# Two layers of the experts: 128-row blocks against 256-row items whose products run in float32r parts

## The chip, the cores and the metric

The kernel runs on one core of a Trainium2 chip, as one launch. The metric is the device time of that launch in microseconds, lower is better. Five engines work beside one another, each on its own list of instructions and joined by semaphores: TensorE (PE in the profile, with its weight loads as PEld), VectorE (DVE), ScalarE (ACT), GpSimd (POOL) and SyncE (SP), which here issues most DMAs.

## The reference, cut to what matters

A decoder layer on 4 batches of 1024 rows with 256 columns, all in float32: self-attention with 16 heads, cross-attention on 77 rows of context, and a mixture of 8 experts of which each row takes its best two. The change is in the experts:

```python
x = x + _L0_attn_ref(_layernorm(x), ...)
x = x + _L0_xattn_ref(_layernorm(x), ctx_1024, ...)
flat_x = _layernorm(x).reshape(-1, 256)          # 4096 rows
logits = flat_x @ W_router + b_router            # 8 experts
top_vals, top_idx = jax.lax.top_k(logits, 2)
for e in range(8):
    h = jax.nn.relu(flat_x @ W1[e] + b1[e])      # W1[e]: 256 x 1024
    y = h @ W2[e] + b2[e]                        # W2[e]: 1024 x 256
    final_output = final_output + y * w[:, None] # w: 0 where the row did not choose e
```

## The kernel before, in words

Attention comes first, batch by batch, and fills TensorE to about 1080 us. Its rows are routed as they are done: the normalised rows are scattered to a table in device memory (`expert_rows`), one region for each expert. 4096 rows with two experts each are 64 blocks of 128 rows when they divide evenly; since each expert rounds up, the kernel has 71 blocks (`NBLK`). The first 40 (`EARLY`) are taken from batches 0 to 2, so that they can run while the second half of batch 3 is still in its cross-attention and routing; a table computed on DVE says for each block which expert and which rows it has.

A block n is these steps, each on one engine:

- `load` (SP): the block's rows into `xi`, and its expert's first weights, 1 MB, into one of three buffers `w1_now`. All eight second weights were brought into `w2` (8 MB) during attention (`prefetch`).
- `xi_turn` (PE), `xi_turned` (ACT): the rows turned, so that columns lie on partitions.
- `up` in two halves (PE): the first layer in plain float32, 32 matmul instructions of 128 columns (one float32 product is two instructions). `hid_fore` (ACT) and `hid_aft` (DVE) add the bias and cut at zero, one half each.
- `down` (PE): the second layer. Blocks 0 to 21 have it in plain float32, 16 instructions of 256 columns. From block 22 (`FINE`) it is a sum of float32r products: a number is split in a high part (rounded to float32r) and the low rest, and high*high + high*low + low*high are summed, 24 instructions of 256 columns. For that `hid_high` (ACT) and `hid_low` (DVE) split the rows, and `w2_high` (ACT) and `w2_low` (DVE) split the weights of each block.
- `yo` (DVE): the product times the row's routing weight, with the bias; `added` (POOL): an indirect DMA that adds 128 rows to the output in device memory. From block 22 POOL computes the routing weight too (`yo_weight`).

The order on each engine is fixed when the kernel is built: the generator `plan()` adds steps to one list, and each engine takes its kinds of steps from it in that order. `TAKES` (line 78) holds the planner's costs of the steps. `blocks()` (line 530) interleaves the steps of blocks n, n+1 and n+2; while batch 3 is being completed, its steps stand between those of `blocks()`. An engine that waits for a semaphore holds everything that stands behind it in its list.

Two kinds of subtraction carry the low parts, both from tensors in SBUF: on DVE (line 1921)

```python
e.tensor_tensor(w2_low[n % NPARTS][:, chunks, :], second_layer(expert, chunks), w2_high[n % NPARTS][:, chunks, :].bitcast(F32), ALU.subtract)
```

and, once at the start of the kernel for 512 columns of the attention weights, on POOL (line 1980, `w_low_late`).

## Time and profile before

| | us |
|---|---|
| median of 3 runs | 1608.52 (1606.69 to 1613.93) |
| profiled execution, first to last instruction | 1607.6 |
| first `xi_turn` (line 1383) | 1081.9 |
| last plain second layer (line 1421) ends | 1274.9 |
| last `yo` (line 1935) starts | 1596.2 |
| `added`, from issue to landing (median, 1300 to 1600 us) | 5.4 |
| PE busy | 1552.3 (97%) |
| DVE busy | 1189.6 (74%) |
| ACT busy | 934.6 (58%) |
| POOL busy | 387.4 (24%) |

The profile page has no time for the profiled execution beside its span; what lies around a span is the difference between the runs' median and it, 0.9 us. The page lists each engine's busy time, and the chain of work that ended last, followed back from the end: 90% of that chain is PE. Stretches of the span can be asked for by window, and each group of instructions by line and shape.

### The profile page before, as it was taken

How to read it: one execution, taken by the hardware profiler on the slowest of the kernel's cores; microseconds unless marked ns; L12 is line 12 of the kernel's file. 1: busy time of each engine (PE TensorE's matmuls, PEld its weight loads, DVE VectorE, ACT ScalarE, POOL GpSimd, SP SyncE). 2: the span in 40 equal slices, each digit the busy share in tenths (PEclk: the TensorE clock that was granted, in tenths of full speed). 3: DMA queues.
4: the chain of work that ended last, by engine and by line, in shares of the span. 5: the costliest groups of instructions: out<-in, count | busy, mean ns of one | idle time of the engine just before them, and what ended most of it. 6: DMA issues, size and time to landing. Idle time of an engine off the chain costs nothing.

```text
span 1607.6 us, 31234 instructions
## 1 busy us (share of the span) xinstructions
PE 1552.3 (97%) x10542; PEld 963.5 (60%) x10542; DVE 1189.6 (74%) x2409; ACT 934.6 (58%) x1786; POOL 387.4 (24%) x462
## 2 busy tenths in 40 slices
PE   5899999999999999999999999999999999999997
PEld 3433443344554444445434443439999999999997
DVE  5888878888877788787877777713354788888885
ACT  3156656677556767664765756772222466666663
POOL 6201120002110041210013100142134334344443
PEclk9799999999999999999999999999999999999998
DMA  6561351232151450314414333234556666766763
GB/s 181 110 126 24 74 122 23 23 43 34 38 99 52 70 86 13 44 41 83 70 51 73 44 106 132 68 130 128 158 179 204 190 199 198 208 191 199 210 192 102
DMA packets 92672, 173.41 MB, mean 108 GB/s; under 512 B 13236, under 2 KB 51124, under 8 KB 92385
## 3 DMA queue, kind: packets, MB, share of 16 engines
q1 hardware_dynamic: 75376, 143.69, 35.2%
q0 software_dynamic: 15744, 26.54, 7.6%
q8 instruction: 85, 1.39, 0.4%
q10 hardware_dynamic: 1392, 1.18, 0.4%
...
## 4 chain that ended last, share of the span: by engine, by line
PE 90%; DVE 4%; ACT 2%; issue 2%; DMA 1%; POOL 0%; SPq 0%; ACTq 0%; DVEq 0%; POOLq 0%
PE ps L1395 16%; PE ps L1183 15%; PE ps L1209 14%; PE ps L1169 13%; PE ps L1138 8%; PE ps L1421 5%; PE ps L1281 2%; PE ps L1315 2%; PE ps L1212 2%; DVE rmax L1632 2%; PE ps L1172 2%; ACT prob L1439 1%; PE ps L1228 1%; PE ps L1383 1%; PE ps L1296 1%
## 5 line engine op out<-in xcount | busy, mean ns | idle before, releaser
L1632 DVE TENSOR_REDUCE rmax<-ps 128x1 f32<-128x512 f32 x960 | 621.2, 685 | 175.4 <-PE ps L1212 86.4
L1439 ACT ACTIVATE prob<-ps 128x512 f32<-128x512 f32 x1024 | 560.8, 601 | 308.2 <-PE ps L1169 157.7
L1209 PE MATMUL ps<-stacked_k,stacked_q 112*128 112x512 bf16 x1024 | 392.1, 390 | 11.4 <-DVE rmax L1629 3.8
L1169 PE MATMUL ps<-stacked_q,stacked_k 115*128 115x512 bf16 x1024 | 358.7, 381 | 3.0 <-ACT prob L1439 1.6
L1183 PE MATMUL ps<-prob,values 128*32 128x512 f32 x2048 | 273.6, 606 | 6.8 <-ACT prob L1439 6.8
L1395 PE MATMUL ps<-xiT,w_now 128*128 128x128 f32 x2272 | 267.5, 275 | 0.0
L1209 PEld LDWEIGHTS ps<-stacked_k,stacked_q 112*128 112x128 bf16 x1024 | 99.5, 99 | 279.2 <-DVE rmax L1632 184.2
L1395 PEld LDWEIGHTS ps<-xiT,w_now 128*128 128x128 f32 x2272 | 262.7, 192 | 1.3
L1169 PEld LDWEIGHTS ps<-stacked_q,stacked_k 115*128 115x128 bf16 x1024 | 97.7, 98 | 152.1 <-ACT prob L1439 67.9
L2060 POOL DMA_INDIRECT out<-yo,xi x71 | 114.9, 1618 | 244.6 <-DVE yo L1935 219.8
L1559 ACT ACTIVATE hidT<-ps,b 128x128 f32<-128x128 f32 x284 | 80.1, 364 | 97.0 <-PE ps L1395 97.0
L1904 DVE TENSOR_SCALAR hidT<-ps,b 128x128 f32<-128x128 f32 x284 | 80.2, 345 | 53.4 <-PE ps L1395 43.8
L1921 DVE TENSOR_TENSOR w_low<-w,w_high 128x2048 fp32r<-128x2048 f32 x49 | 112.3, 2293 | 5.9 <-issue 4.3
L1138 PE MATMUL ps<-w_high,hid_high 128*128 128x256 f32 x392 | 114.1, 291 | 0.0
L1569 ACT ACTIVATE hid_high<-hidT 128x512 fp32r<-128x512 f32 x98 | 62.1, 634 | 89.4 <-DVE hidT L1904 87.7
L1212 PE MATMUL ps<-ramps,slopes 128*128 128x128 f16 x512 | 113.3, 221 | 0.0
L1172 PE MATMUL ps<-ramps,slopes 128*128 128x128 f16 x512 | 112.4, 219 | 0.0
L1138 PE MATMUL ps<-w_high,hid_low 128*128 128x256 f32 x392 | 110.1, 281 | 0.0
L1138 PE MATMUL ps<-w_low,hid_high 128*128 128x256 f32 x392 | 110.1, 281 | 0.0
L1581 ACT ACTIVATE w_high<-w 128x2048 fp32r x49 | 93.7, 1913 | 16.8 <-issue 15.8
L1961 POOL TENSOR_TENSOR rstd_of<-varp,minus_half 128x8 f32<-128x8 f32 (+1 forms) x14 | 21.3, 1520 | 333.4 <-DVE varp L1680 333.4
L2020 POOL DMA_INDIRECT expert_rows<-xn,slot x64 | 62.1, 971 | 160.9 <-ACT prob L1439 128.6
...
## 6 DMA issues: line engine op xcount, KB each, us to landing
w_now<-in_w SPq DMA_DIRECT2D x71, 1024.0 KB, 5.3
...
w<-in_w SPq DMA_DIRECT2D x8, 1024.0 KB, 9.2
...
xr<-in_x POOLq DMA_DIRECT2D x4, 1024.0 KB, 9.8
```

The source lines that it names most:

```text
L1138: last = e.matmul(ps[:, bank, 0:D], rows[n % 2][:, c, :], weights[n % NPARTS][:, c, :], start=(c == 0 and i == 0), stop=(c == FC - 1 and i ...
L1169: m = e.matmul(ps[:, bank, :], ka[i][0:ROWS, hh, kt * P:(kt + 1) * P], qa[i][0:ROWS, hh, ch * BANK:(ch + 1) * BANK], start=True, stop=True)
L1172: m = e.matmul(ps[:, bank, (kt % 4) * P:(kt % 4 + 1) * P], slopes[:, g * HG + hh, :], ramps[:, kt % 2, :], start=False, stop=True, skip_gr ...
L1183: m = e.matmul(ps[CT * hh:CT * (hh + 1), AV_BANK, :], vt[b % 2][:, kt, c0:c0 + CT], prob[:, unit_of(G, ch, kt, hh) % NPROB, :], start=(kt ...
L1209: m = e.matmul(ps[:, bank, :], qa[i][0:MAX_ROW, hh, qt * P:(qt + 1) * P], ka[i][0:MAX_ROW, hh, kc * BANK:(kc + 1) * BANK], start=True, sto ...
L1212: m = e.matmul(ps[:, bank, (qt % 4) * P:(qt % 4 + 1) * P], slopes[:, g * HG + hh, :], ramps[:, 1 - qt % 2, :], start=False, stop=True, ski ...
L1395: m = e.matmul(ps[:, 1 + 2 * (n % 2) + half, q * P:(q + 1) * P], w1_now[n % NW][:, c, f * P:(f + 1) * P], xiT[n % 2][:, c, :], start=(c == ...
L1439: e.activation(prob[:, u % NPROB, :], ps[:, score_bank(u), :], ACT.Exp).then_inc(sem["exp"], 1)
L1581: e.activation(w2_high[n % NPARTS][:, :, :], second_layer(expert, slice(0, FC)), ACT.Copy).then_inc(sem["w2_high"], 1)
L1632: e.tensor_reduce(rmax[:, G % 2, hh * NT + qt, kc:kc + 1], ps[:, p.bank("max", *k), :], AX.X, ALU.max).then_inc(sem["maxed"], 1)
L1921: e.tensor_tensor(w2_low[n % NPARTS][:, chunks, :], second_layer(expert, chunks), w2_high[n % NPARTS][:, chunks, :].bitcast(F32), ALU.subt ...
L2060: e.indirect_dma_start(t["out"], bass.IndirectOffsetOnAxis(ap=xi[n % NX][:, TOKEN:TOKEN + 1].bitcast(I32), axis=0), yo[n % NY][:, :], None ...
```

## The change

The 71 blocks become 39 items: 32 of 256 rows (pairs) and 7 of 128 rows (singles). Items 0 to 16 are pairs and are taken from batches 0 to 2; of the other 22, items 20, 23, 26, 29, 32, 35 and 38 are singles. In a pair both layers are sums of three float32r products: `up` is four quarters of 12 instructions with 256 columns, `down` is 24 instructions of 256 columns for each of its two tiles. The split of the rows before the first layer is new (`xi_high` on ACT, `xi_low` on DVE, 128x512 each), and so is the split of the first weights (`w1_high` on ACT, `w1_low` on POOL, 128x2048 each, for every pair). `hid_high` and `hid_low` cover 128x1024 in one instruction, `hid_fore` and `hid_aft` 128x256. A single has both layers in plain float32 and splits nothing. The second weights are no longer prefetched; each item loads its 1 MB of first and 1 MB of second weights (3 and 2 buffers). The weights lie in device memory so that a partition reads 8 KB in one piece. `yo` computes the routing weight itself on DVE for every tile, and POOL's `yo_weight` is gone. The table step on DVE is rewritten for pairs and singles.

```diff
+NX, NY, N1, N2, NH2 = 4, 2, 3, 2, 2
...
+EARLY = -(-((NB - 1) * S * TOPK - NE * (PAIR - 1)) // PAIR)
+LATE = NBLK - 2 * EARLY
+SINGLES = NE - 1
+PAIRS_LATE = (LATE - SINGLES) // 2
+assert 2 * PAIRS_LATE + SINGLES == LATE
...
+    tiles, unit = [2] * EARLY, [2 * n for n in range(EARLY)]
+    pairs, singles = iter(range(PAIRS_LATE)), iter(range(SINGLES))
+    for n in range(PAIRS_LATE + SINGLES):
+        alone = n % 3 == 0 and n > 0
+        tiles.append(1 if alone else 2)
+        unit.append(2 * EARLY + (2 * PAIRS_LATE + next(singles) if alone else 2 * next(pairs)))
+    return tiles, unit
...
+    def split_first(n):
+        if TILES[n] == 2:
+            add("w1_high", n)
+            add("w1_low", n)
...
+    def split_second(n):
+        if TILES[n] == 2:
+            add("w2_high", n)
+            add("w2_low", n)
...
+    def up_quarter(n, q):
+        add("up", n, q)
+        add(("hid_fore", "hid_aft")[q % 2], n, q)
...
     def blocks():
-        turn_block(0)
-        turn_block(1)
+        split_first(0)
+        turn_item(0)
         yield
-        for half in range(2):
-            up_half(0, half)
+        split_first(1)
+        turn_item(1)
+        yield
+        for q in range(4):
+            up_quarter(0, q)
+            if q % 2:
+                split_rows(0, q // 2)
             yield
-        for n in range(NBLK):
-            if n + NW < NBLK:
-                add("load", n + NW)
-            if n + 1 < NBLK:
-                for half in range(2):
-                    up_half(n + 1, half)
-                    if n + 1 >= FINE and half == 0:
+        add("load_1", N1)
+        split_second(0)
+        split_first(2)
+        for n in range(NITEM):
+            for q in range(4):
+                if n + 1 < NITEM:
+                    up_quarter(n + 1, q)
+                    if q == 1:
                         split_rows(n + 1, 0)
                     yield
-            if n + 2 < NBLK:
-                turn_block(n + 2)
-            if FINE <= n + NPARTS - 1 < NBLK and n + 1 > FINE:
-                add("w2_low", n + NPARTS - 1)
-            if FINE <= n + 1 < NBLK:
+            if n + 4 < NITEM:
+                assert n + 4 != EARLY or ("table", 1, TABLE_PARTS - 1) in p.number
+                add("load_1", n + 4)
+            if n + 2 < NITEM:
+                turn_item(n + 2)
+            if n + 1 < NITEM:
                 split_rows(n + 1, 1)
-            add("down", n)
-            add("yo", n)
-            if FINE <= n + 1 < NBLK:
-                assert n == FINE - 1 or ("table", 1, TABLE_PARTS - 1) in p.number
-                add("yo_weight", n + 1)
-            if n == NBLK - 1:
-                add("last_front")
-            add("added", n)
-            if FINE <= n + NPARTS < NBLK:
-                assert ("scatter", NB - 1, NT - 1, TOPK - 1) in p.number
-                add("w2_high", n + NPARTS)
-                if n + NPARTS < FINE + 2:
-                    add("w2_low", n + NPARTS)
-            yield
+            if n + 3 < NITEM:
+                split_first(n + 3)
+            for tt in range(TILES[n]):
+                add("down", n, tt)
+                if tt == 0 and n + 1 < NITEM:
+                    split_second(n + 1)
+                yield
+            for tt in range(TILES[n]):
+                add("yo", n, tt)
+                add("added", n, tt)
+            if n + 2 < NITEM:
+                add("load_2", n + 2)
+            if n + NX < NITEM:
+                assert n + NX != EARLY or ("zeros", NE - 1) in p.number
+                add("load_x", n + NX)
...
+                elif kind == "load_1":
+                    n, = k
...
+                    if n == 2:
+                        e.wait_ge(sem["attend"], attend_of(LAST, NCH - 1, NT - 1))
+                    elif n >= N1:
+                        e.wait_ge(sem["up"], p.upto("up", n - N1, 3))
+                    of = e.value_load(expert_of[0:1, UNIT[n]:UNIT[n] + 1], min_val=0, max_val=NE - 1)
+                    e.dma_start(w1_now[n % N1][:, :, :], t["w1"][bass.ds(of, 1)].rearrange("a p c f -> p (a c) f")).then_inc(sem[f"w1_in{n % N1}"], 16)
+                elif kind == "load_2":
+                    n, = k
+                    if n >= N2:
+                        e.wait_ge(sem["down"], p.upto("down", n - N2, last_tile(n - N2)))
+                    of = e.value_load(expert_of[0:1, UNIT[n]:UNIT[n] + 1], min_val=0, max_val=NE - 1)
+                    e.dma_start(w2_now[n % N2][:, :, :], t["w2"][bass.ds(of, 1)].rearrange("a p c f -> p (a c) f")).then_inc(sem[f"w2_in{n % N2}"], 16)
+                elif kind == "load_x":
...
                         landed(e, n - NX)
-                    at = e.value_load(row_of[0:1, n:n + 1], min_val=0, max_val=NROW - P)
-                    e.dma_start(xi[n % NX][:, :], rows_in[bass.ds(at, P), :]).then_inc(sem[f"slots_in{n % NX}"], 16)
-                    if n >= NW:
-                        e.wait_ge(sem["up"], p.upto("up", n - NW, 1))
-                    if n >= 2:
-                        first_layer(n)
+                    for tt in range(TILES[n]):
+                        at = e.value_load(row_of[0:1, UNIT[n] + tt:UNIT[n] + tt + 1], min_val=0, max_val=IDLE)
+                        e.dma_start(xi[n % NX][tt][:, :], rows_in[bass.ds(at, P), :]).then_inc(sem[f"slots_in{n % NX}"], 16)
 
         @block.tensor
         def _(e):
-            def down_in_parts(n, bank):
...
+                    if q == 0 and TILES[n] == 2:
+                        e.wait_ge(sem["xi_low"], p.upto("xi_low", n))
+                        e.wait_ge(sem["w1_low"], p.upto("w1_low", n))
+                    elif q == 0:
+                        e.wait_ge(sem["xi_high"], p.upto("xi_high", n))
+                        e.wait_ge(sem[f"w1_in{n % N1}"], 16 * (n // N1 + 1))
+                    for f in (2 * q, 2 * q + 1):
+                        cols = slice(f * P, (f + 1) * P)
+                        into = ps[:, 1 + q, f % 2 * PAIR:f % 2 * PAIR + TILES[n] * P]
                         for c in range(DC):
-                            m = e.matmul(ps[:, 1 + 2 * (n % 2) + half, q * P:(q + 1) * P], w1_now[n % NW][:, c, f * P:(f + 1) * P],
-                                         xiT[n % 2][:, c, :], start=(c == 0), stop=(c == DC - 1))
+                            if TILES[n] == 2:
+                                high, low = xT_high[n % 2][:, c, :], xT_low[n % 2][:, c, :]
+                                e.matmul(into, w1_high[n % NH2][:, c, cols], high, start=(c == 0), stop=False)
+                                e.matmul(into, w1_high[n % NH2][:, c, cols], low, start=False, stop=False)
+                                m = e.matmul(into, w1_low[n % N1][:, c, cols], high, start=False, stop=(c == DC - 1))
+                            else:
+                                m = e.matmul(into, w1_now[n % N1][:, c, cols], xT_one[n % 2][:, c, :], start=(c == 0), stop=(c == DC - 1))
                     m.then_inc(sem["up"], 1)
...
+                    if TILES[n] == 2:
+                        if tt == 0:
+                            e.wait_ge(sem["w2_low"], p.upto("w2_low", n))
+                        for c in range(FC):
+                            if tt == 0 and c % (FC // 2) == 0:
+                                e.wait_ge(sem["hid_low"], p.upto("hid_low", n, c // (FC // 2)))
+                            high, low = hid_high[n % 2][:, c, tile_of(tt)], hid_low[n % 2][:, c, tile_of(tt)]
+                            e.matmul(into, high, w2_high[n % NH2][:, c, :], start=(c == 0), stop=False)
+                            e.matmul(into, high, w2_low[n % N2][:, c, :], start=False, stop=False)
+                            m = e.matmul(into, low, w2_high[n % NH2][:, c, :], start=False, stop=(c == FC - 1))
                     else:
...
+                elif kind == "w1_high":
+                    n, = k
...
+                    e.wait_ge(sem[f"w1_in{n % N1}"], 16 * (n // N1 + 1))
+                    if n >= NH2:
+                        e.wait_ge(sem["up"], p.upto("up", n - NH2, 3))
+                    e.activation(w1_high[n % NH2][:, :, :], w1_now[n % N1][:, :, :], ACT.Copy).then_inc(sem["w1_high"], 1)
...
+                elif kind == "xi_low":
+                    n, = k
+                    e.wait_ge(sem["xi_high"], p.upto("xi_high", n))
+                    rows = ps[:, 0, 0:DC * PAIR].rearrange("p (c r) -> p c r", c=DC)
+                    e.tensor_tensor(xT_low[n % 2][:, :, :], rows, xT_high[n % 2][:, :, :].bitcast(F32), ALU.subtract).then_inc(sem["xi_low"], 1)
...
+                    e.tensor_tensor(w2_low[n % N2][:, :, :], w2_now[n % N2][:, :, :], w2_high[n % NH2][:, :, :].bitcast(F32),
                                     ALU.subtract).then_inc(sem["w2_low"], 1)
...
-                elif kind == "yo_weight":
+                elif kind == "w1_low":
...
+                    e.wait_ge(sem["w1_high"], p.upto("w1_high", n))
+                    e.tensor_tensor(w1_low[n % N1][:, :, :], w1_now[n % N1][:, :, :], w1_high[n % NH2][:, :, :].bitcast(F32),
+                                    ALU.subtract).then_inc(sem["w1_low"], 1)
...
+                    e.wait_ge(sem["yo"], p.upto("yo", n, tt))
+                    if tt == 0 and n:
                         landed(e, n - 1)
-                    e.indirect_dma_start(t["out"], bass.IndirectOffsetOnAxis(ap=xi[n % NX][:, TOKEN:TOKEN + 1].bitcast(I32), axis=0),
-                                         yo[n % NY][:, :], None, compute_op=ALU.add).then_inc(sem[f"added{n % 2}"], 16)
-            landed(e, NBLK - 2)
-            landed(e, NBLK - 1)
+                    e.indirect_dma_start(t["out"], bass.IndirectOffsetOnAxis(ap=xi[n % NX][tt][:, TOKEN:TOKEN + 1].bitcast(I32), axis=0),
+                                         yo[n % NY][tt][:, :], None, compute_op=ALU.add).then_inc(sem["landed"], 16)
+            landed(e, NITEM - 1)
 
```

The lists of three engines show the change in the steady part. First DVE, between one split of second weights and the next; before, `w2_low` is line 1921, `hid_low` 1913, `yo` 1935 and the 128x128 rows of 1904 are `hid_aft`:

```order
L1921 TENSOR_TENSOR w2_low2<-w2,w2_high2 128x2048
L1913 TENSOR_TENSOR hid_low1<-hidT1,hid_high1 128x512
...
L1933 TENSOR_SCALAR bias0<-b2_all,weight0 128x256
L1935 SCALAR_TENSOR_TENSOR yo0<-ps,weight0,bias0 128x256
L1913 TENSOR_TENSOR hid_low0<-hidT0,hid_high0 128x512
...
L1904 TENSOR_SCALAR hidT0<-ps,b1 128x128
...
L1904 TENSOR_SCALAR hidT0<-ps,b1 128x128
...
L1904 TENSOR_SCALAR hidT0<-ps,b1 128x128
...
L1904 TENSOR_SCALAR hidT0<-ps,b1 128x128
...
L1921 TENSOR_TENSOR w2_low0<-w2,w2_high0 128x2048
```

Now, over one pair (`hid_aft` is line 1981, `hid_low` 1988, `xi_low` 1969, `w2_low` 1993, `yo` with its bias 2005 and 2007):

```order
L1981 TENSOR_SCALAR hid0<-ps,b1 128x256
...
L1981 TENSOR_SCALAR hid0<-ps,b1 128x256
L1988 TENSOR_TENSOR hid_low0<-hid0,hid_high0 128x1024
...
L1981 TENSOR_SCALAR hid0<-ps,b1 128x256
...
L1981 TENSOR_SCALAR hid0<-ps,b1 128x256
L1969 TENSOR_TENSOR xT_low1<-ps,xT_high1 128x512
L1988 TENSOR_TENSOR hid_low0<-hid0,hid_high0 128x1024
L1993 TENSOR_TENSOR w2_low0<-w2_now0,w2_high0 128x2048
...
L2005 TENSOR_SCALAR bias0<-b2_all,weight0 128x256
L2007 SCALAR_TENSOR_TENSOR yo10<-ps,weight0,bias0 128x256
...
L2005 TENSOR_SCALAR bias1<-b2_all,weight1 128x256
L2007 SCALAR_TENSOR_TENSOR yo11<-ps,weight1,bias1 128x256
```

The split of the second weights stood ahead of the last split of the rows; now it is behind both, directly ahead of the two `yo` of the item before. Then ACT, before (`hid_fore` 1559, `hid_high` 1569, `xi_turned` 1545, `w2_high` 1581):

```order
L1569 ACTIVATE hid_high1<-hidT1 128x512
L1545 ACTIVATE xiT0<-ps 128x256
L1569 ACTIVATE hid_high1<-hidT1 128x512
...
L1581 ACTIVATE w2_high0<-w2 128x2048
...
L1559 ACTIVATE hidT0<-ps,b1 128x128
...
L1559 ACTIVATE hidT0<-ps,b1 128x128
...
L1559 ACTIVATE hidT0<-ps,b1 128x128
...
L1559 ACTIVATE hidT0<-ps,b1 128x128
L1569 ACTIVATE hid_high0<-hidT0 128x512
L1545 ACTIVATE xiT1<-ps 128x256
L1569 ACTIVATE hid_high0<-hidT0 128x512
```

and now, from one `w2_high` (line 1627) to the next, with `w1_high` 1621, `hid_fore` 1640, `hid_high` 1648 and `xi_high` 1612:

```order
L1627 ACTIVATE w2_high0<-w2_now0 128x2048
...
L1640 ACTIVATE hid1<-ps,b1 128x256
...
L1640 ACTIVATE hid1<-ps,b1 128x256
L1648 ACTIVATE hid_high1<-hid1 128x1024
...
L1640 ACTIVATE hid1<-ps,b1 128x256
...
L1640 ACTIVATE hid1<-ps,b1 128x256
L1612 ACTIVATE xT_high0<-ps 128x512
L1648 ACTIVATE hid_high1<-hid1 128x1024
L1621 ACTIVATE w1_high1<-w1_now0 128x2048
L1627 ACTIVATE w2_high1<-w2_now1 128x2048
```

Two conversions of 128x2048 stand behind one another, first the first weights of the item two further on, then the second weights of this one. Last POOL, the end of its list before (`added` is line 2060, the routing weight 1591 to 1595):

```order
L2060 DMA out<-yo1,xi0 4224x256
...
L1591 TENSOR_SCALAR weight1<-xi2,code_of 128x1
L1592 TENSOR_TENSOR weight1<-weight1,xi2 128x1
L1595 TENSOR_TENSOR weight1<-weight1,xi2 128x1
L2060 DMA out<-yo0,xi1 4224x256
```

and now the first pairs (`w1_low` is line 2098, `added` 2112, 2033 and 2083 belong to batch 3):

```order
L2098 TENSOR_TENSOR w1_low0<-w1_now0,w1_high0 128x2048
L2098 TENSOR_TENSOR w1_low1<-w1_now1,w1_high1 128x2048
L2083 TENSOR_TENSOR xr<-xr,xbo_all 128x256 x4
L2098 TENSOR_TENSOR w1_low2<-w1_now2,w1_high0 128x2048
L2033 TENSOR_TENSOR rstd_of0<-varp0,minus_half 128x4
L2098 TENSOR_TENSOR w1_low0<-w1_now0,w1_high1 128x2048
L2112 DMA out<-yo00,xi00 4224x256
L2112 DMA out<-yo01,xi01 4224x256
L2083 TENSOR_TENSOR xr<-xr,xbo_all 128x256 x4
L2098 TENSOR_TENSOR w1_low1<-w1_now1,w1_high0 128x2048
L2112 DMA out<-yo10,xi10 4224x256
L2112 DMA out<-yo11,xi11 4224x256
```

A 128x2048 subtraction per pair has come into POOL's list, ahead of the two `added` of an item.

## Rows read from the trace of the kernel before

**Rows 1.** Page, part 1: busy us (share of the span) and instructions.

```profile
PE 1552.3 (97%) x10542; PEld 963.5 (60%) x10542; DVE 1189.6 (74%) x2409; ACT 934.6 (58%) x1786; POOL 387.4 (24%) x462
```

**Rows 2.** Chain that ended last, in order of time: start us, us, what.

```profile
1216.89 3.57 PE ps L1395 x32
1220.68 3.46 PE ps L1421 x16
1224.14 3.57 PE ps L1395 x32
...
1298.54 2.84 PE ps L1138 x24
1301.38 3.57 PE ps L1395 x32
1305.17 2.84 PE ps L1138 x24
```

**Rows 3.** Windows: length, then busy us (instructions) by engine, clock, DMA share, GB/s.

```profile
1110.00:1270.00 160.00, 160.00 (x1102) 150.00 (x1102) 75.58 (x291) 43.69 (x122) 51.57 (x41) 1.00 0.60 179
1300.00:1400.00 100.00, 100.00 (x877) 100.00 (x876) 82.57 (x138) 67.15 (x120) 42.34 (x63) 1.00 0.67 199
```

**Rows 4.** Groups by line and shape, ACT: xcount, busy us, mean ns, idle before.

```profile
L1581 ACT ACTIVATE w_high<-w 128x2048 fp32r x49 | 93.7, 1913 | 16.8 <-issue 15.8 <-PE ps L1138 0.9
...
L1569 ACT ACTIVATE hid_high<-hidT 128x512 fp32r<-128x512 f32 x98 | 62.1, 634 | 89.4 <-DVE hidT L1904 87.7
```

**Rows 5.** The same for DVE.

```profile
L1921 DVE TENSOR_TENSOR w_low<-w,w_high 128x2048 fp32r<-128x2048 f32 x49 | 112.3, 2293 | 5.9 <-issue 4.3
L1904 DVE TENSOR_SCALAR hidT<-ps,b 128x128 f32<-128x128 f32 x284 | 80.2, 345 | 53.4 <-PE ps L1395 43.8 <-issue 5.2 <-DVE landed_of L1890 0.9
L1913 DVE TENSOR_TENSOR hid_low<-hidT,hid_high 128x512 fp32r<-128x512 f32 x98 | 67.7, 691 | 44.2 <-ACT hid_high L1569 44.2
```

**Rows 6.** Timeline of DVE around one `yo`: start us, us, instruction.

```profile
1105.49 1.13 DVE L1904 TENSOR_SCALAR hidT<-ps,b 128x128 f32<-128x128 f32 x4 [1.08 <-PE ps L1395]
...
1106.55 0.22 DVE L1588 SCALAR_TENSOR_TENSOR weight<-xi,code_of 128x1 f32<-128x1 f32 x1
...
1107.12 0.35 DVE L1933 TENSOR_SCALAR bias<-b_all,weight 128x256 f32 x1 [0.15 <-DVE weight L1595]
...
1109.09 0.48 DVE L1935 SCALAR_TENSOR_TENSOR yo<-ps,weight,bias 128x256 f32<-128x256 f32 x1 [1.62 <-PE ps L1421]
```

**Rows 7.** Line 1607 on POOL: duration ns min/median/max, first and last start.

```profile
L1607 POOL TENSOR_TENSOR q_part<-rest_of,q_part x14: 1152/1157/1167, 34.3 to 717.8; 128x512 bf16<-128x512 f32 x14
```

**Rows 8.** Line 2006 on POOL, 256 columns, same columns.

```profile
L2006 POOL TENSOR_TENSOR xr<-xr,bo_all x32: 711/728/739, 226.7 to 1076.4; 128x256 f32<-128x256 f32 x32
```

**Rows 9.** Line 1607 on DVE, same columns.

```profile
L1607 DVE TENSOR_TENSOR q_part<-rest_of,q_part x2: 693/694/694, 21.4 to 27.0; 128x512 bf16<-128x512 f32 x2
```

**Rows 10.** Line 1592 on POOL, one column wide, same columns.

```profile
L1592 POOL TENSOR_TENSOR weight<-weight,xi x49: 189/190/2290, 1276.8 to 1593.0; 128x1 f32<-128x1 f32 x49
```

**Rows 11.** Timeline at 27 us, POOL and DVE at once.

```profile
27.11 3.17 POOL L1980 TENSOR_TENSOR wqkv_low<-xn,wqkv_high 128x512 fp32r<-128x512 f32 x2
...
29.16 1.67 DVE L1607 TENSOR_TENSOR k_part<-rest_of,k_part 128x512 bf16<-128x512 f32 x1
```

**Rows 12.** Timeline at 1340 us, DVE and POOL at once.

```profile
1340.86 2.29 DVE L1921 TENSOR_TENSOR w_low<-w,w_high 128x2048 fp32r<-128x2048 f32 x1
...
1340.92 2.28 POOL L1592 TENSOR_TENSOR weight<-weight,xi 128x1 f32<-128x1 f32 x1
```

**Rows 13.** Windows where attention ends and the blocks begin, columns as in rows 3.

```profile
1076.00:1082.00 6.00, 3.19 (x22) 2.23 (x18) 0.75 (x3) 3.14 (x6) 1.08 (x2) 1.00 0.39 79
1082.00:1090.00 8.00, 7.53 (x46) 6.81 (x44) 0.69 (x1) 2.88 (x8) 2.78 (x4) 0.79 0.38 140
```

**Rows 14.** DMA from 1300 to 1600 us: queue and loads to landing.

```profile
q1 hardware_dynamic: 17874, 50.80, 49.3%
...
w_now<-in_w SPq DMA_DIRECT2D x43, 1024.0 KB, 5.4
```

506 lines of the change are left out of this document (242 added, 264 removed).

## The prediction

> **What bounds the kernel now.** I read the busy times first: PE works 97% of the span, DVE 74%, ACT less [rows 1]. That is a mean over two parts, so I asked for windows in the part that changes. From 1300 to 1400 us PE is busy without a gap and at full clock, DVE 83 of 100 us, ACT 67 [rows 3]. The chain of waits there is PE alone, and its starts repeat: 7.25 us for a block with a plain float32 second layer (1216.89 to 1224.14), 6.63 us for one with float32r parts (1298.54 to 1305.17) [rows 2]. So 22 blocks of 7.25 and 49 of 6.63 make 484 us, and every us that PE is spared is gained as long as PE stays the engine waited for. DVE has only 17 us in 100 to spare.
>
> **PE: what is removed.** A float32r product with 256 columns takes 2.84 / 24 = 0.118 us [rows 2]. A pair has 48 of them for each layer and four turning products of about 0.11 (what lies between a first layer's end and the second's start: 1305.17 - 1301.38 - 3.57 = 0.22 for two): 96 x 0.118 + 0.44 = 11.8 us, against 14.5 for two early blocks and 13.3 for two late ones. A single is the old plain block, 7.25. Sum 32 x 11.8 + 7 x 7.25 = 428 us, **56 us less** than 484. That holds only if the others deliver a pair in 11.8 us.
>
> **Do they? The loop through DVE, ACT and POOL.** The lists are in order, so I follow them from the end of one item's last `yo` to the end of the next item's, and price each step.
>
> - `hid_aft` quarter 1 of the next item but one, two instructions of 256 columns. One of 128 takes 0.345, four 1.13 [rows 5, 6], so the spacing is 0.26; DVE needs (2293 - 691) / 1536 = 1.04 ns for a column [rows 5], so 128 more columns cost 0.13: 0.39 + 0.48 = 0.9 us.
> - `hid_high` of half 0 waits for it: 128x1024 on ACT, 0.634 + 512 x 0.833 ns (from 634 and 1913 ns) [rows 4] = 1.06.
> - `hid_low` of half 0 waits for that: 0.69 + 0.53 = 1.22 [rows 5].
> - `hid_aft` quarter 3, behind it on DVE: 0.9.
> - `hid_high` of half 1: 1.06. On DVE `xi_low` runs beside it.
> - `w1_high`, 128x2048 behind it on ACT: 1.91 [rows 4].
> - `w1_low` on POOL waits for that; its price is below, 4.6.
> - `w2_low` on DVE, 2.29 [rows 5]. It needs `w2_high`, which follows `w1_high` on ACT and takes 1.91, but I have it wait for `w1_low`.
> - two `yo` behind it: 0.92 from the start of the weight to the end of the bias, then 0.48 [rows 6]: 2 x 1.4 = 2.8.
>
> Sum 16.7; six hand-overs at some 0.05 make **17.0 us for a pair, against PE's 11.8**. `down` of the next item waits for the last `yo`, as DVE reads the same PSUM bank, so PE stands still for 5.2 us in each. Behind the blocked `w2_low` stand both `yo` and the `hid_aft` of the item after; POOL's `added` waits for the `yo`.
>
> **Why `w2_low` waits for `w1_low`.** No semaphore joins them. But both subtract two tensors in SBUF. At 29.16 us a DVE subtraction of this kind took 1.67 us while POOL's ran (27.11 to 30.28), where the same form takes 0.69 [rows 9, 11]. At 1340.92 us a POOL instruction on one column, usually 0.19 us, took 2.28 and ended together with a DVE `w2_low` started just before [rows 10, 12]. So whoever starts second stands still for the whole of the other. `w1_low` starts when `w1_high` ends, 1.91 us ahead of `w2_high`'s end, so POOL is always first.
>
> The Trainium skill, SBUF — State Buffer, section Who interferes with whom, states this as a rule against such a pair: a DVE instruction with two SBUF inputs contends with a GpSimd instruction that reads SBUF, by an exclusive lock for the whole instruction. By that rule `w2_low` waits as above and the sum is the one given; without it the loop is the 14.3 us of the second rival. The trace agrees, by the two cases shown.
>
> **The price of `w1_low`.** Before has no POOL subtraction over 2048 columns. From 0.73 for 256 and 1.16 for 512 columns [rows 7, 8] the slope gives 1.16 + 1536 x 1.68 ns = 3.7 us; four times the 512-column instruction is 4.6; four times half of the 3.17 us in [rows 11], disturbed by DVE, is 6.3. I take 4.6, scaled from the nearest undisturbed form; 3.7 and 6.3 are the ends. The skill's GPSIMD Engine Reference, section Elementwise — side-by-side cycle accounting, gives 4.5 us for a tensor_tensor of 2048 float32 columns; by it the sum would be 2 us less.
>
> **How often the loop is paid.** An interval is from one item's `down` to the next one's.
> - Items 1 to 17 and 19: 18 intervals of 17.0 instead of 11.8: +93.6.
> - Items 22, 25, 28, 31, 34: behind them a single runs its first layer, so PE would need 3.57 + 0.22 + 5.68 = 9.5; the loop still holds, as `w1_low` of item n+2 is in it: 5 x 7.5 = +37.5.
> - Items 18 and 37 have no `w1_low` in the loop (20 and 39 are a single and none): 17.0 - 4.6 = 12.4, +0.6 and +2.9.
> - The singles and the items behind them are PE-bound, 9.5 and 11.5 us.
> Together **+135 us**.
>
> **The smaller terms.**
> - Batch 3's tail. Before, PE goes from 1081.9 to about 1275 for 22 blocks, 193 - 159.5 = 34 us of it for the tail. That now lies in PE's gaps. But DVE has the tail's work in the loop: 75.6 us in [rows 3] less 20 blocks of 2.5 (1.13 + 0.92 + 0.48 [rows 6]) is 25, and the part before 1110 about 6; ACT adds a few. 31 and more against 34: I take 0, within -20 and +15, as part of it can lie in DVE's wait for `w1_low`.
> - Start. The first `up` also waits for `w1_high` and `w1_low` of item 0, 1.9 + 4.6 us, partly beside batch 3: +3.5; filling with 256 rows instead of 128 another 2.5. **+6**.
> - Clock. After attention PE had 3.19 of 6 us busy, and the granted clock was 0.79 in the next 8 us [rows 13], that is 3.4 us at the lower of two levels, 1.2 and 2.4 GHz. In a run of pairs a slow phase of up to 10 us is eaten by the 5.2 us gap. Behind the six gaps of 7.5 PE-bound items follow: 6 x 1.7 = **+10**.
> - Weights and DMA: hidden. A pair brings 2.36 MB; queue 1 moved 50.80 MB in 300 us at a 49.3% share, 343 GB/s when busy [rows 14], so 6.9 us and about 2 to land (5.4 for a load of 1 MB, which moves in 3.1), in 17. `load_x` holds SP's list until an item has landed, 2.3 us for two `added` and 5.4 for the landing behind the last `yo`; `load_1` behind it lands by 15, and is wanted at 22. If that cover went, `w1_high` would be late by the difference.
> - The 8 MB no longer fetched during attention, POOL's routing weights gone, the new table step: nothing waits for them; 0 within 2.
>
> **Sum.** -56 + 135 + 0 + 6 + 10 = +95 us. 1607.6 + 95 = 1702.6 for the profiled execution, and the runs' median lies 0.9 above its span: **1703 us**.
>
> **Rivals.**
> 1. *The two subtractions don't block each other.* Then `w2_low` follows `w2_high`: 17.0 - 4.6 + 1.9 = 14.3 us, 2.7 less in 23 intervals, 62 us: 1641. Against it stand both cases in rows 11 and 12. Chance 0.10.
> 2. *PE stays the bound, the other side.* All 135 us fall away where the loop is under 11.8 us; the kernel gets faster once it is below about 13.0, as 23 intervals then give back less than 56 - 6 - 10 = 40 us or so. It would need `w1_low` and one more 128x2048 conversion outside the loop, if `yo` or `hid_aft` overlapped more than the in-order lists let them. 1607.6 - 56 + 6 = 1558. For it speaks only that ACT and DVE by busy time fit (about 8 and 10 us of 11.8). Chance 0.05.
> 3. *Something else is longer still.* Loads of two queues collide and `w1_high` is late, or PE falls to 1.2 GHz for whole pairs: 2 x 11.8 = 23.6 us against 17.0, 6.6 us in each interval where it lasts; in ten of them 1770. Against it: the loads' 7 us of slack, and that the gap covers a slow phase of 10 us. Chance 0.04.
> 4. The loop half hidden, within 0.5% of before: 0.02.
> My forecast has 0.79. With `w1_low` at 3.7, 0.9 x 23 = 21 us less, 1682; at 6.3, 39 more, 1742. Its own range is 1675 to 1742; for 8 in 10 with the first rival the range is **1640 to 1742**. 0.5%, 8 us, is what a measurement here can tell from no change: faster 0.05, same 0.02, slower 0.93.
>
> **What would show it.** In the new profile: `w2_low` (line 1993) lasts 4.6 - 1.9 + 2.3 = 5.0 us in the mean where it follows a `w1_low`, and 2.29 in the others; `w1_low` (line 2098) 4 to 5 us; two successive early `down` stand 17 us apart, three late items take 38; PE waits for DVE's `yo`, and is busy 11.8 of 17 us; the clock is below 1 in the part of the experts. Wrong I would be if `w2_low` stayed at 2.3 us (first rival), if PE were still busy all the time (second), or if the chain of waits ran over DMA or a slow clock (third).

## The result, and the profile after

The changed kernel takes 1743.16 us (median of 4 runs, 1741.30 to 1743.76) against 1610.32 for the kernel before beside it (1606.69 to 1613.93): a ratio of 1.083, 95% interval [1.080, 1.085]. The profiled execution has a span of 1739.2 us. It is slower, as forecast, by the mechanism that the forecast named; but 1703 was too low by 40 us, and the measured time lies 1 us above the range. Of the 40 us, 37 lie between the spans of forecast and profiled execution; the rest is that the profiled execution was the fastest of the four, and that 2.1 us lie around its span instead of 0.9.

First the busy times, which answer to [rows 1], and the granted clock in 40 slices:

```profile
PE 1553.7 (89%) x10150; PEld 963.7 (55%) x10150; DVE 1283.3 (74%) x2377; ACT 940.8 (54%) x1607; POOL 474.7 (27%) x346
...
PEclk9899999999999999999999999888888899899998
```

TensorE went from 97% to 89% of a longer span. DVE's share is still 74%: an average that shows nothing of a loop. What TensorE waits for stands in the view of waits from 1110 us to the end (waiter, what it waited for, total us, times, longest):

```profile
ACT hid_high L1648 <- DVE hid L1981: 203.4, 54, 11.4
...
POOL w_low L2098 <- ACT w_high L1621: 133.4, 22, 11.6
...
PE ps L1477 <- DVE yo L2007: 82.0, 17, 7.5
DVE w_low L1993 <- ACT w_high L1627: 59.0, 30, 2.5
```

PE stands idle for 137 us in this stretch (629 less 491.6 of work). 82 of them are `down` behind the `yo` of the item before (57 of the 69 us idle from 1380 us on); some 33 are waits of batch 3's own steps. The chain of waits inside one steady item (start, duration, what) goes through the steps that the forecast lists:

```profile
1380.29 0.32 DVE yo L2007
...
1381.47 0.49 DVE hid L1981
1382.05 1.06 ACT hid_high L1648
1383.13 0.34 DVE hid_low L1988
...
1384.28 0.88 DVE hid L1981 x2
1385.37 0.84 issue
1386.21 1.90 ACT w_high L1621
1388.11 1.81 ACT w_high L1627
1389.94 0.34 DVE w_low L1993
1390.31 0.19 DVEq L2000
1390.56 4.34 issue
1394.90 0.22 DVE weight L2002
```

The 4.34 us called "issue" are the rest of `w2_low`, its stall with it: no semaphore is waited for, and the profile has no name for the stall. In the timelines of POOL and DVE the two subtractions are:

```profile
1388.19 4.64 POOL L2098 TENSOR_TENSOR w_low<-w_now,w_high 128x2048 fp32r<-128x2048 f32 x1 [5.36 <-ACT w_high L1621]
...
1389.94 5.03 DVE L1993 TENSOR_TENSOR w_low<-w_now,w_high 128x2048 fp32r<-128x2048 f32 x1 [2.38 <-ACT w_high L1627]
```

`w1_low` ends at 1392.83, `w2_low` 2.14 us later: about 2.9 us stand still, the rest is its own work. The view by line shows the same on all items, against 2293 ns in [rows 5]; `w1_low` is the new POOL group:

```profile
L2098 POOL TENSOR_TENSOR w_low<-w_now,w_high 128x2048 fp32r<-128x2048 f32 x29 | 136.6, 4709 | 133.4 <-ACT w_high L1621 133.4
...
L1993 DVE TENSOR_TENSOR w_low<-w_now,w_high 128x2048 fp32r<-128x2048 f32 x31 | 131.9, 4254 | 59.0 <-ACT w_high L1627 59.0
```

### The profile page after: what moved, and what is told of

It reads as the page before. It is cut to its first block, busy times and chain, and to the rows that moved or that the text cites. A ratio compares the mean times of both kernels' runs of the same rounds, so it can differ in the third digit from the quotient of the medians.

```text
span 1739.2 us, 28911 instructions
## 1 busy us (share of the span) xinstructions
PE 1553.7 (89%) x10150; PEld 963.7 (55%) x10150; DVE 1283.3 (74%) x2377; ACT 940.8 (54%) x1607; POOL 474.7 (27%) x346
## 4 chain that ended last, share of the span: by engine, by line
PE 61%; DVE 14%; issue 10%; ACT 9%; DMA 3%; DVEq 2%; POOL 0%; SPq 0%; ACTq 0%; POOLq 0%
PE ps L1234 14%; PE ps L1260 13%; PE ps L1220 12%; ACT w_high L1627 3%; DVE w_low L1993 2%; ACT w_high L1621 2%; DMA w_now<-in_w 2%; DVE rmax L1685 2%; DVE hid L1981 2%; PE ps L1263 2%; PE ps L1366 2%; PE ps L1332 2%; PE ps L1223 2%; ACT prob L1502 1%; ACT hid_high L1648 1%
## 5 line engine op out<-in xcount | busy, mean ns | idle before, releaser
L2098 POOL TENSOR_TENSOR w_low<-w_now,w_high 128x2048 fp32r<-128x2048 f32 x32 | 150.5, 4706 | 148.1 <-ACT w_high L1621 148.1
L1648 ACT ACTIVATE hid_high<-hid 128x1024 fp32r<-128x1024 f32 x64 | 67.7, 1058 | 217.6 <-DVE hid L1981 209.9
L1993 DVE TENSOR_TENSOR w_low<-w_now,w_high 128x2048 fp32r<-128x2048 f32 x32 | 134.2, 4192 | 59.3 <-ACT w_high L1627 59.3
L2112 POOL DMA_INDIRECT out<-yo,xi x71 | 110.7, 1559 | 199.3 <-DVE yo L2007 191.1
L1477 PEld LDWEIGHTS ps<-w_high,hid_high 128*128 128x128 f32 x512 | 114.9, 224 | 86.4 <-DVE yo L2007 86.4
L1457 PE MATMUL ps<-xT_high,w_high 128*128 128x256 f32 x512 | 152.3, 297 | 10.0 <-issue 7.9
L1459 PE MATMUL ps<-xT_high,w_low 128*128 128x256 f32 x512 | 148.4, 290 | 0.0
L1458 PE MATMUL ps<-xT_low,w_high 128*128 128x256 f32 x512 | 148.2, 289 | 0.0
L1988 DVE TENSOR_TENSOR hid_low<-hid,hid_high 128x1024 fp32r<-128x1024 f32 x64 | 83.1, 1298 | 59.4 <-ACT hid_high L1648 58.2
L1478 PEld LDWEIGHTS ps<-w_low,hid_high 128*128 128x128 f32 x512 | 114.6, 224 | 0.0
L1479 PEld LDWEIGHTS ps<-w_high,hid_low 128*128 128x128 f32 x512 | 114.0, 223 | 0.0
```

Of the source, the lines that this page charges most:

```text
L1457: e.matmul(into, w1_high[n % NH2][:, c, cols], high, start=(c == 0), stop=False)
L1459: m = e.matmul(into, w1_low[n % N1][:, c, cols], high, start=False, stop=(c == DC - 1))
L1477: e.matmul(into, high, w2_high[n % NH2][:, c, :], start=(c == 0), stop=False)
L1478: e.matmul(into, high, w2_low[n % N2][:, c, :], start=False, stop=False)
L1479: m = e.matmul(into, low, w2_high[n % NH2][:, c, :], start=False, stop=(c == FC - 1))
L1993: e.tensor_tensor(w2_low[n % N2][:, :, :], w2_now[n % N2][:, :, :], w2_high[n % NH2][:, :, :].bitcast(F32), ALU.subtract).then_inc(sem["w2 ...
```

## The forecast against the trace, stretch by stretch

The last `yo` of an item is a good mark, since all of the loop passes it. In the timeline of DVE they start here for item 0, item 12 and item 38:

```profile
1124.89 0.48 DVE L2007 SCALAR_TENSOR_TENSOR yo<-ps,weight,bias 128x256 f32<-128x256 f32 x1
...
1380.29 0.48 DVE L2007 SCALAR_TENSOR_TENSOR yo<-ps,weight,bias 128x256 f32<-128x256 f32 x1
...
1727.90 0.48 DVE L2007 SCALAR_TENSOR_TENSOR yo<-ps,weight,bias 128x256 f32<-128x256 f32 x1 [4.15 <-PE ps L1485]
```

In the kernel before, the same rows (of block 1 and block 25, the second halves of these items) are:

```profile
1109.09 0.48 DVE L1935 SCALAR_TENSOR_TENSOR yo<-ps,weight,bias 128x256 f32<-128x256 f32 x1 [1.62 <-PE ps L1421]
...
1304.61 0.48 DVE L1935 SCALAR_TENSOR_TENSOR yo<-ps,weight,bias 128x256 f32<-128x256 f32 x1
```

| stretch | by the forecast's terms | measured | off by |
|---|---|---|---|
| item 0 | 1109.1 - 2.7 (one pair's gain) + 6 = 1112.4 | 1124.9 | +12.5 |
| items 1 to 12 | 12 x 17.0 + 24 of tail = 228 | 255.4 | +27.4 |
| items 13 to 38 | 343 + 10 for the clock | 347.6 | -5 |
| behind the last `yo` | 9.2 (what is left of 1702.6) | 11.3 | +2 |

The kernel before has 11.4 us behind its last `yo` (1607.6 - 1596.2), so the forecast's terms for the other stretches are 2 us short in all, and the last row is no error of its own. The 24 us of tail are what batch 3 costs before in this stretch: 195.5 us for 24 blocks less 20 x 7.25 and 4 x 6.63. So the steady part was forecast within 2%: pairs of 17.2 us where 17.0 stood, groups of three of 39.4 in the mean where 38 stood. The error lies in the first thirteen items, and is to be explained by the start and the tail of batch 3.

## Experiments

Each edit is to the changed kernel unless it says otherwise. Ratios are to the kernel before (1608 to 1611 us when measured beside them). "The port" is a name for what POOL and DVE contend for; no view shows it, only that one of the two stands still.

**1 and 2: is it the port, and is it the reading?** (The code is cut. In e2 TensorE reads the 512 columns for all products.)

```diff
-e.tensor_tensor(w1_low[...], w1_now[...], w1_high[...].bitcast(F32), ALU.subtract).then_inc(...)
+then(e.memset(w1_low[n % N1][:, :, :].bitcast(F32), 0.0))      # e1; three writes, 4.66 us in all
+then(e.memset(w1_low[n % N1][:, :, :].bitcast(F32), 0.0))
+e.memset(w1_low[n % N1][:, 0, :].bitcast(F32), 0.0).then_inc(sem["w1_low"], 1)
+e.tensor_tensor(w1_low[:, 0, 0:512], w1_now[:, 0, 0:512], w1_high[:, 0, 0:512]...)   # e2
```

> GpSimd's subtraction w1_low is replaced by three writes of a constant into the same buffer (2048, 2048 and 1024 columns, together about 4.5 us by the 1799 ns of a 2048-column memset in the trace), so POOL works as long as before but reads nothing from SBUF; the low part of W1 is left out. Everything else, the semaphores and the lists too, is as in the changed kernel. Theory (DVE's subtraction stands still while a POOL instruction reads two tensors in SBUF): w2_low lasts 2.3 us in the mean instead of 4.2, a pair takes 14.3 us instead of 17.2, the time falls by about 62 to 65 us, to 1678 (1668 to 1690). Rival 1 (w2_low is slow or late for another reason: its own form, ACT's conversion, a semaphore): w2_low stays at 4 to 5 us, time 1743 within 5. Rival 2 (any long POOL instruction blocks DVE, by its write): w2_low stays at about 4.9 us, time 1743.

> w1_low on POOL subtracts 512 instead of 2048 columns, about 1.16 us instead of 4.6; TensorE reads those 512 columns for all products, so its work is unchanged (three quarters of the low part of W1 are left out). Theory (blocked subtraction in the loop): w1_low ends before w2_high does, w2_low lasts 2.3 us, a pair takes 14.3 us, 1676 (1666 to 1690), the same as with the write-only POOL work although POOL is now short. Rival (POOL's length matters by itself, by added or bias2 behind it in its list): clearly below the write-only kernel, by 10 us or more. Rival (neither): 1743.

Measured: e1 1681.4 us, ratio 1.044 [1.040, 1.048]; e2 1677.0, 1.041 [1.039, 1.044]. The rows of e1:

```profile
L1993 DVE TENSOR_TENSOR w_low<-w_now,w_high 128x2048 fp32r<-128x2048 f32 x31 | 71.1, 2293 | 58.8 <-ACT w_high L1627 58.8
...
L2099 POOL MEMSET w_low<- 128x2048 f32 x29 | 54.9, 1894 | 130.1 <-ACT w_high L1621 130.1
L2100 POOL MEMSET w_low<- 128x2048 f32 x29 | 52.6, 1814 | 1.7
L2101 POOL MEMSET w_low<- 128x1024 f32 x29 | 27.6, 953 | 1.7
```

POOL was as busy as in the changed kernel (1894 + 1814 + 953 = 4661 ns for an item, against 4709), and no `w2_low` took more than 2294 ns. Both theories that kept it at 4 to 5 us fall, "any long POOL instruction" with them. Without the block the changed kernel is 62 to 66 us faster; the forecast's rival had 62.

**3: the other order.**

```diff
-            if n + 3 < NITEM:
-                split_first(n + 3)
             for tt in range(TILES[n]):
                 add("down", n, tt)
                 if tt == 0 and n + 1 < NITEM:
                     split_second(n + 1)
                 yield
+            if n + 3 < NITEM:
+                split_first(n + 3)
```

> Nothing left out. The split of W1 for item n+3 is listed after the split of W2 for item n+1 and both down, ahead of the yo: ACT converts w2 first, so DVE's w2_low starts 1.9 us ahead of POOL's w1_low and is not blocked. Theory (who starts first goes through, the other waits): w2_low 2.3 us, a pair about 12.7 us, the time falls by some 80 us to 1662 (1650 to 1680); now hid_low or w1_low shows stretched instances. Rival (DVE always loses against POOL, or time is divided): w2_low still over 4 us and the time above 1700.

Measured 1736.0, 1.078 [1.075, 1.080]: 7 us less, not 80. `w2_low` was freed as expected (2434 ns in the mean), but the block went on to the next DVE instruction that reads two tensors in SBUF, the weight of `yo`, one column wide:

```profile
L2002 DVE SCALAR_TENSOR_TENSOR weight<-xi,code_of 128x1 f32<-128x1 f32 x71 | 106.6, 1501 | 8.9 <-issue 6.9 <-DVE chosen L1829 0.7 <-DVE slot L1862 0.7
```

In its timeline of DVE and then of POOL the two end together, at 1407.12 and 1407.11, though the one usually takes 0.22 us:

```profile
1402.55 4.57 DVE L2002 SCALAR_TENSOR_TENSOR weight<-xi,code_of 128x1 f32<-128x1 f32 x1
...
1402.19 4.92 POOL L2098 TENSOR_TENSOR w_low<-w_now,w_high 128x2048 fp32r<-128x2048 f32 x1 [7.16 <-ACT w_high L1621]
```

My expectation had looked only at the subtractions. That the one who starts first goes through stands; my list of what it applies to was too short.

**5: is DVE's tail work in the loop?**

```diff
-for n in range(V):
-    then(e.tensor_tensor(end[:, n + 1:n + 2], end[:, n:n + 1], width[:, n:n + 1], ALU.add))
+for again in range(8 if which else 1):
+    for n in range(V):
+        then(e.tensor_tensor(end[:, n + 1:n + 2], end[:, n:n + 1], width[:, n:n + 1], ALU.add))
```

> On the changed kernel: in the second table step the chain of 16 one-column additions on DVE (3.06 us in the trace after) is done eight times, to the same result: 7 x 3.06 = 21.4 us more on DVE at one place of batch 3's tail. Theory (DVE's list is in the loop, so the tail's DVE work, the new table step with it, adds fully): 1743 + 21 = 1764 (1760 to 1767). Rival (the tail's DVE work lies in DVE's waits for ACT or POOL): 1743 to 1750. By the same rule the table step as it is (about 10 us of DVE in one interval, 27.8 against 17.2 us) costs about 10 us of the changed kernel.

Measured 1763.6, 1.097 [1.095, 1.099]: +20.4 us for 21.7 us of DVE. The chain, in the kernel after and with the edit:

```profile
1323.63 3.06 DVE L1919 TENSOR_TENSOR end<-end,width 128x1 f32<-128x1 f32 x16
```

```profile
1323.77 24.77 DVE L1920 TENSOR_TENSOR end<-end,width 128x1 f32<-128x1 f32 x128
```

The item's interval went from 27.8 to 49.4 us and none of the other first twenty moved by more than 1. So DVE work at this place of the tail adds one for one; other places were not tested. In the kernel after, the interval with the table step is 27.8 between neighbours of 19.0 and 18.9: the step costs 8.8 us.

**6: is it the clock?**

```diff
 elif tt == 0:
+    if n + 1 < NITEM:
+        e.wait_ge(sem["hid_fore"], p.upto("hid_fore", n + 1, 0))
+        for _ in range(12):
+            e.matmul(ps[:, 1, 0:P], ident[:, :], ident[:, :], start=True, stop=True)
     e.wait_ge(sem["yo"], p.upto("yo", n - 1, last_tile(n - 1)))
```

> On the changed kernel: TensorE does 12 more float32 products of 128x128 (about 2.6 us, written to a bank that nobody reads) ahead of each item's down, in the 5 us in which it otherwise waits for DVE's yo. Theory (the drops of the granted clock behind the gaps cost 10 us and more, above all in batch 3's tail, where the clock is 0.84 to 0.87): the clock rises to 0.95 or more, the time falls by 10 to 25 us. Rival (the slow phases are hidden in the gaps, the loop over DVE, ACT and POOL sets the time alone): within 5 us of 1743; where TensorE has no gap (singles) the products even add some 2.6 us each, 14 items, up to +30.

Measured 1746.7, 1.086 [1.084, 1.088]. The mean clock over the span rose from 0.949 to 0.971. In the windows from 1300 to 1400 (start:end, us, then PE, PEld, DVE, ACT and POOL busy with their counts, clock, DMA share, GB/s), after and then with the edit:

```profile
1300.00:1400.00 100.00, 72.85 (x507) 71.49 (x507) 74.06 (x130) 39.00 (x46) 48.30 (x22) 0.84 0.52 152
```

```profile
1300.00:1400.00 100.00, 81.23 (x620) 79.93 (x620) 74.10 (x131) 38.53 (x45) 48.03 (x23) 0.90 0.52 153
```

Steady pairs stayed at 17.2 us, the intervals of items 9 to 13 moved by 0.1 us at most, and the time did not fall. So in this stretch TensorE's slow phases lie in its gaps. That the clock reached 0.90 here and not 0.95 leaves a part of it untested. In the late part it rose from 0.91 to 0.99 (1450 to 1720 us), and items 13 to 38 took 351.1 us instead of 347.6; but there the added products themselves take TensorE's time beside the singles, so what the clock alone costs there is not separated.

**7 and 9: how long does POOL keep the port?**

```diff
-                    e.tensor_tensor(w1_low[...] (2048 columns), ..., ALU.subtract).then_inc(sem["w1_low"], 1)
+                    for c in range(DC):
+                        for h in range(2):
+                            f = slice(h * 512, (h + 1) * 512)
+                            m = e.tensor_tensor(w1_low[n % N1][:, c, f], ...)          # e7
+                            then(m)   # e9; the last one signals w1_low instead
 (lists: w1_high between the two down; w2_high behind both; w1_low and w2_low behind yo and added)
```

> Nothing left out. w1_low in four POOL instructions of 512 columns, listed behind added; w1_high between the two down on ACT, w2_high behind both, w2_low on DVE behind the yo (a whole item ahead of its use). Theory (a POOL instruction that reads SBUF holds the port for its own length, DVE gets it between two of them; no instruction of the loop waits for a w1_low of 4.6 us): steady pairs 12 to 13 us, three late items 32 to 34 us, in all 90 to 106 us less: 1637 to 1655. Rival (POOL keeps the port from one instruction to the next of a row, so that quarters are no better than one): pairs at 14.2 us, about 1675. Rival 2 (the four instructions take longer together, 1.4 instead of 1.16 each as the 512-column one with DVE's disturbance): 1650 to 1665.

> Nothing left out. As e7 (w1_low in four POOL instructions, w2_low behind the yo), but each POOL instruction waits for the end of the one before it, so that POOL stands still for a moment between two of them. In e7 a DVE subtraction issued behind the first quarter ended only after the fourth (5.59 us). Theory (POOL keeps the port over a row of instructions that follow without a gap, and a gap gives it to DVE): hid_low at most 2.6 us, pairs 12 to 14 us, time 1714 - 35 to 60 = 1655 to 1680. Rival (a waiting DVE instruction isn't let in for another reason, a gap changes nothing): hid_low stays at 5.6 us, time 1710 to 1720.

Measured: e7 1714.4, 1.066 [1.062, 1.069], above all that I expected, its rival's 1675 too; e9 1663.0, 1.035 [1.033, 1.037]. One `hid_low` in e7, then the same one in e9:

```profile
1409.55 5.59 DVE L1995 TENSOR_TENSOR hid_low<-hid,hid_high 128x1024 fp32r<-128x1024 f32 x1 [1.19 <-ACT hid_high L1655]
```

```profile
1403.94 1.86 DVE L1995 TENSOR_TENSOR hid_low<-hid,hid_high 128x1024 fp32r<-128x1024 f32 x1 [1.19 <-ACT hid_high L1655]
```

The four quarters on POOL, in e7 and then in e9:

```profile
1408.45 5.60 POOL L2108 TENSOR_TENSOR w_low<-w_now,w_high 128x512 fp32r<-128x512 f32 x4
```

```profile
1402.84 7.70 POOL L2108 TENSOR_TENSOR w_low<-w_now,w_high 128x512 fp32r<-128x512 f32 x4
```

In e7 the quarters follow each other without a gap; DVE's subtraction, 1.22 us by itself, waits 4.4 us and gets through only behind the fourth. In e9 each quarter waits for the end of the one before, and DVE gets in at the next gap: it takes 1.86. POOL then stretches instead, 7.7 us for its four. A pair went from 15.9 to 13.6 us. So the mechanism of e7's rival and the theory of e9 hold: instructions that stand ready in POOL's queue share one hold of the port. Not the rival's price: it had 14.2 us for a pair. In e9 a pair has 12.2 us of TensorE work at a clock of 0.98 (36.5 us for three, from 1344 to 1386), which agrees with the forecast's 11.8 at full clock.

**4, 8, 10 and 11: without the split of W1.** e4 takes the first layer of a pair as a plain float32 product; e8 adds two banks and a later place for the rows' loads; e10 is e4 with W2's split placed earlier and the loads right behind `load_1`; e11 is e10 with two banks.

```diff
+def in_parts_of(n):
+    return TILES[n] == 2 and False                      # e4; used for xi_low, w1_high, w1_low, up
+down_bank = lambda n: NSCORE + NMAX if n >= 14 and n % 2 else AV_BANK       # e8, e11
             if n + 4 < NITEM:
                 add("load_1", n + 4)
+            if n and n + NX - 1 < NITEM:                  # e10, e11; in e8 behind load_2
+                add("load_x", n + NX - 1)
+            w2_high, w2_low of n + 1                      # e10, e11: ahead of turn_item(n + 2)
```

> Nothing left out. Pairs as before, the second layer in float32r parts, but the first layer of a pair as a plain float32 product straight from the loaded W1: no w1_high, w1_low, xi_low. TensorE then needs 6.8 + 0.4 + 5.7 = 13.0 us a pair and no loop is longer. Theory: steady pairs 13.0 us, three late items 33.1 us, batch 3's tail no longer behind w1_low on POOL, so item 0's last yo ends about 20 us earlier than in the changed kernel; 1743 - 110 to 130 = 1613 to 1633, about level with the kernel before (1610). Rival (start and tail cost come from the pairs and their in-order lists and not from the W1 split): the start stays within 5 us of the changed kernel's and the time is above 1640.

> Nothing left out. As the kernel with a plain first layer and a second layer in parts (1653.8), and from item 14 on down alternates between two PSUM banks, so that it waits for the yo of the item but one; the rows of an item are loaded one item later in the list, so that SP's list isn't held by the landing of the last output. Theory (the late part of that kernel, 36 us for three items instead of 33.1, waits for the yo of a single and for loads behind the landing): 25 to 30 us less than 1653.8 for 8 groups of three and some clock: 1625 to 1632. Rival (something else, ACT or DVE in their lists): 1645 to 1654.

> Nothing left out. As e4 (first layer of a pair plain, 1653.8), with the split of W2 listed ahead of the turning products, so that DVE's w2_low fills its wait for hid_high, and with an item's rows loaded behind load_1 instead of behind load_2. Theory (DVE's and ACT's list is the loop in batch 3's tail, and SP's list holds loads behind a landing in the late part): tail about 10 us shorter, late part up to 15 shorter: 1630 to 1645. Rival (it is TensorE's own list, which waits for each step of the tail in turn): within 5 us of 1654.

> Nothing left out. As e10, and down alternates between two PSUM banks from item 14 on. Theory (the late part's 3 us a group of three are TensorE's wait for the yo of a single before it): 8 groups by 2 to 3 us, 16 to 24 us less than e10: about 1615 to 1625, within 1% of the kernel before. Rival (loads and list order alone): as e10 within 4 us.

| kernel | us | ratio | item 0's last `yo` | items 1 to 12 | pair |
|---|---|---|---|---|---|
| after | 1743.2 | 1.083 [1.080, 1.085] | 1124.9 | 255.4 | 17.2 |
| e4 | 1653.8 | 1.027 [1.025, 1.030] | 1114.1 | 211.6 | 13.0 |
| e8 | 1672.1 | 1.038 [1.036, 1.041] | 1115.6 | 212.6 | 13.0 |
| e10 | 1625.0 | 1.013 [1.010, 1.016] | 1114.0 | 194.1 | 11.3 to 13.1 |
| e11 | 1620.1 | 1.010 [1.007, 1.012] | 1114.3 | 193.7 | 11.3 to 13.1 |

e4: 89 us less, and item 0 is 11 earlier, so part of the start was the W1 split; but 20 us of the expected gain were missing, because the tail cost as much as before (next section). e8 missed, and in the wrong direction: TensorE then waited for the rows, whose load stood behind a `load_2` that waits for a `down`:

```profile
PE ps L1445 <- DMA xi<-expert_rows: 21.4, 9, 4.1
```

e10 mended that place: 29 us less than e4. TensorE is nearly full again from 1300 to 1500 us (e10; e4 had 93.24 and 94.13):

```profile
1300.00:1400.00 100.00, 98.78 (x649) 92.43 (x649) 67.43 (x119) 43.80 (x63) 24.81 (x16) 1.00 0.71 210
1400.00:1500.00 100.00, 100.00 (x654) 93.52 (x653) 61.20 (x115) 40.20 (x64) 23.28 (x15) 1.00 0.75 230
```

The two banks give 5 us or less (e11 against e10: the intervals of the ratios overlap), where I expected 16 to 24, and 4 of them lie in the last item alone (6.0 us in e10, 1.9 in e11); so e4's late part was not held by the bank but, as e10's gain has it, by list order and loads. e10 changed two placements at once: of the 34 us between the profiled executions of e4 and e10, 18 lie in items 1 to 12 and 16 behind them, but which placement gave how much stays open. No version beat the kernel before: e11 is slower by 1.0%, 0.7 to 1.2.

## Why the forecast was right in direction and too low

**Right: the loop.** The path through DVE, ACT and POOL, `w1_low` at 4.6 (measured 4.71) and `w2_low` at 5.0 behind it (5.03 in the item shown) held, and gave 17.2 us a pair. TensorE's sum of 11.8 holds for full clock (e9); in the changed kernel it was busy 13.7 of 17.1 us, at a granted clock of 0.90, where I had written 11.8 of 17. In the runs the rule that was weighed there (the Trainium skill, SBUF — State Buffer, section Who interferes with whom) was confirmed on both sides: with POOL reading, 4254 ns in the mean; with POOL writing only, 2293. Where that section has the hold end with the instruction, e7 shows more: four instructions that stood ready held it to the end of the last one. The price for `w1_low` in the Trainium skill (GPSIMD Engine Reference, section Elementwise — side-by-side cycle accounting, 4.5 us) agrees with the median of 4.62 us (4.52 to 5.21).

**The step that failed: batch 3's tail, "I take 0, within -20 and +15".** It cost 25 us more than that: 49 us between the marks, as added up below, where the forecast's terms have 24. (The other 2.4 of the 27.4 are twelve pairs of 17.2 instead of 17.0.) I set 34 us that the tail cost before against 31 us of DVE work that it would cost now. Three things were wrong in this difference. It was the difference for the whole tail, though 10 of the 34 us lie ahead of block 1 and so ahead of the loop; between the marks only 24 go. It took the table step to cost what it did before: the 31 us hold the old step with 6.1 us of DVE, the new one has 11.4, and I had written that nothing waits for it. Its interval is 8.8 us longer than its neighbours, and e5 shows that DVE work there adds fully. And it hoped that part of DVE's tail work would lie in DVE's wait for `w1_low`. Grouped by line, DVE's work in this stretch that belongs to no item is 34.4 us, with 4.4 of idle time directly ahead of it: 39 us. Some of the groups, from 1125 to 1380:

```profile
L1725 DVE BATCH_NORM_STATS2 stats_of<-xr 128x6 f32<-128x256 f32 x8 | 3.2, 417 | 0.0
...
L1789 DVE TENSOR_TENSOR xr<-ps,xr 128x512 f32<-128x512 f32 x4 | 2.7, 684 | 1.2 <-PE ps L1367 1.2
```

The twelve intervals sum to 255.4 - 12 x 17.2 = 49 us above the steady pair. The same excess stands in kernels with quite different pairs: e1 225.1 - 12 x 14.8 = 47.5, e2 224.3 - 12 x 14.4 = 51.5, e3 252.4 - 12 x 17.0 = 48.4, e4 211.6 - 12 x 13.0 = 55.6. So it needs neither the block nor the W1 split. It does move with the order of the lists: e7 has 248.3 - 12 x 15.9 = 57.5 and e9 225.8 - 12 x 13.6 = 62.6, and e10, which differs from e4 in placements alone, is 17.5 us shorter in this stretch. 39 of the 49 us are as long as DVE's tail work in its list. That they are this work is shown for the table step (e5) and argued for the rest; against a plain sum speaks e4, which has 55.6 although its steady pairs of 13.0 us are set by TensorE. That the other 10 are TensorE and ACT steps of the tail, each waited for in turn, is argued from the 26.3 us for which PE stood idle ahead of tail instructions, and not tested.

**The second: "Start, +6".** Item 0 was 12.5 us later still. POOL does `w1_low` of items 0 and 1 in one row and only then the additions of `xbo` for batch 3's tail, but no engine's wait is put down to them. The third row, on DVE, is the `w2_low` of item 1, which stands ahead of item 0's `yo`:

```profile
1083.36 9.05 POOL L2098 TENSOR_TENSOR w_low<-w_now,w_high 128x2048 fp32r<-128x2048 f32 x2 [6.59 <-ACT w_high L1621]
1092.34 2.87 POOL L2083 TENSOR_TENSOR xr<-xr,xbo_all 128x256 f32<-128x256 f32 x4
...
1116.11 4.91 DVE L1993 TENSOR_TENSOR w_low<-w_now,w_high 128x2048 fp32r<-128x2048 f32 x1 [2.38 <-ACT w_high L1627]
```

I had counted item 0's `w1_low` alone. With `w1_low` a quarter as long (e2), item 0's last `yo` starts at 1116.2 instead of 1124.9, 8.7 us earlier. 1.1 of them lie ahead of the items already: the first `w1_high` starts at 1080.24 instead of 1081.38. Some 3.8 come up to the first `hid_aft`, from the `up` that waits for `w1_low`; the forecast's +6 holds them as 3.5. The other 3.7 are stalls that it left out: a `hid_low` of 2.29 us (1.23 in e2) and the `w2_low` shown, 4.91 (2.29 in e2). So some 4 of the 12.5 us are explained, and some 9 are not.

**The third, the other way: clock, +10.** Items 13 to 38 were 5 us under the forecast with these 10 and 5 above it without, so the clock cost them 5 us at most; e6 does not separate it there.

12.5 + 27.4 - 5 + 2 = 37 us, the difference between the two spans, 1739.2 and 1702.6. The range's upper end, 1742, was set by the price of `w1_low` alone. The bounds of the tail, +15, and of the start stood in the text but were never added to it.
